# Self attentions of a two-block decoder: split low-precision products against fp32 products with 32 rows a head

## The chip, the cores and the metric

The kernel runs on one core of one Trainium2 chip. The metric is the device time of one launch in microseconds. The engines named below are TensorE (PE, matmuls and transposes; PEld is its weight load), VectorE (DVE), ScalarE (ACT), GpSimd (POOL) and SyncE (SP, which issues most transfers).

## The reference

Two decoder blocks over x of 8 batches x 256 tokens x 256 features, each sublayer followed by a layer norm of the sum with its input: a gated convolution block, a cross attention to 77 context rows, a mixture of experts; then a self attention with rotary positions, a second cross attention, and a last attention with register tokens. The change touches the self attention and the last attention. Both have 16 heads of 16 features.

```python
def _L1_attn_ref(x, w_qkv, w_out, b_out):
    q, k, v = ...                       # (b, 16, 256, 16)
    q, k = _apply_rope(q, cos, sin), _apply_rope(k, cos, sin)
    attn = softmax(einsum('bhsd,bhtd->bhst', q, k) * SCALE)
    return einsum('bhst,bhtd->bhsd', attn, v)... @ w_out + b_out

def _L1_ffn_ref(x, g_info, W_qkv, W_proj, b_proj):
    sim = (qg_n * q_n).sum(-1).mean(-1)           # of the tokens past the first REG = 5
    pos = (sim - sim.min()) / (sim.max() - sim.min()) > 0.9
    def masked_attn(tok_mask):
        l = where(concat([ones(REG), tok_mask]), logits, -inf)
        return einsum('bhqk,bkhd->bqhd', softmax(l), v)
    x_pos, x_neg = masked_attn(pos), masked_attn(~pos)
    reg_out = (x_pos[:, :REG] + x_neg[:, :REG]) * 0.5
    tok_out = where(pos, x_pos[:, REG:], x_neg[:, REG:])
    return concat([reg_out, tok_out]) @ W_proj + b_proj
```

## The kernel before, in words

Even and odd batches are two streams with buffers and four PSUM banks each. `pair(st, i)` is two banks of a stream, `bank(st, i)` one. Every engine's program is written as Python generators, one per stream, and `together` and `beside` (lines 103 to 116) take one piece from each generator in turn. A `yield` or `pause(n)` is the end of a piece, so the places of the yields set the order of each engine's instructions. Engines wait for each other through counted signals with named steps (`sig.up` and `at`). The work goes in stages: x0 (first block up to its cross attention), experts, then `second` for each batch of a stream (`a1`, the self attention; `xattn`; `fq`, which makes queries, keys and values of the last attention and sends them to DRAM), and `fa`, the last attention. Four pairs of batches pass through `second`, then through `fa`.

The self attention `a1` (PE from line 865, ACT 1205, DVE 1596). TensorE turns x, makes queries, keys and values with `mm3` (lines 92 to 95: three products of fp32r high and low parts), VectorE applies the rotation (L1327). `stack` (a ScalarE copy of the high parts, L1006, then VectorE's subtraction for the low parts) lays high and low parts side by side, 48 numbers per head, and one more for minus the row's maximum. TensorE turns two heads at a time (`turn`, transposes at L544), ScalarE copies the result from PSUM. Then `maxima` (L805) multiplies without the maximum, VectorE reduces 128 x 1024 numbers at a time (L1338) and the queries are turned again with the maximum in place. `weigh` takes four groups of two heads for each half of the heads: scores with keys on the partitions (L830), two exponentials of the same scores (L1195 to f16, L1196 to fp32), the low part by subtraction on VectorE (L1327), and 16 small bf16 matmuls with the weights stationary and the values, in three bf16 pieces, moving (L847, L848). VectorE sums the pieces (L1338), inverts and multiplies. `project` turns the result and multiplies with the output weights.

The last attention `fa` (PE 976, ACT 1303, DVE 1748) does the same with two more rows per head for the mask: query and key carry a row of marks each, so that a token sees only its own kind. The five register tokens need both masks. Their second query is made as a block diagonal of 8 columns a head, with maxima (L946), scores (L957, L959), an exponential pair and value products (L971, L972) of their own. `front`, the stacks and turns of the next pair, is interleaved into `weigh` on all three engines.

Lines for prices named later: L606 is an fp32 projection of the context, L662 an fp32 score product of the cross attention in column tiles of 64.

## Time and profile before

| | us |
|---|---|
| median of 3 runs | 2320.46 (2318.49 to 2326.34) |
| the profiled execution | 2325.29, span 2323.5 |
| TensorE matmuls busy | 1759.7 (76%), 12736 records |
| VectorE busy | 1172.5 (50%) |
| ScalarE busy | 918.3 (40%) |
| GpSimd busy | 431.9 (19%) |
| mean granted TensorE clock | 0.792 of full speed |

The profiled execution lies 4.8 us above the median. Its page has a line of 40 slices in which the granted clock is 7 tenths or more in all but one of the first twenty, and 5 to 8 tenths in nineteen of the last twenty (from 1160 us on), which are the rest of the self attention, second cross attention and last attention. A row of the timeline is a run of like instructions: "x16" after a row says that it stands for sixteen, and the bracket names the idle time before it and what ended that. Busy time of TensorE overlaps from one matmul to the next, so spacing of starts is the better measure of its pace.

### The profile page before, as it was taken

How to read it: one execution, taken by the hardware profiler on the slowest of the kernel's cores; microseconds unless marked ns; L12 is line 12 of the kernel's file. 1: busy time of each engine (PE TensorE's matmuls, PEld its weight loads, DVE VectorE, ACT ScalarE, POOL GpSimd, SP SyncE). 2: the span in 40 equal slices, each digit the busy share in tenths (PEclk: the TensorE clock that was granted, in tenths of full speed). 3: DMA queues.
4: the chain of work that ended last, by engine and by line, in shares of the span. 5: the costliest groups of instructions: out<-in, count | busy, mean ns of one | idle time of the engine just before them, and what ended most of it. 6: DMA issues, size and time to landing. Idle time of an engine off the chain costs nothing.

```text
span 2323.5 us, 30395 instructions
## 1 busy us (share of the span) xinstructions
PE 1759.7 (76%) x12736; PEld 1506.3 (65%) x12736; DVE 1172.5 (50%) x2262; ACT 918.3 (40%) x1115; POOL 431.9 (19%) x375
## 2 busy tenths in 40 slices
PE   6685886858799999995686688668767837666666
PEld 6575775656688888884575576557556736555555
DVE  3354443554353333336743754384256436768577
ACT  2443423334322333222641643363236334553735
POOL 1210200102223444432023012302211130000000
PEclk9887888878889999997598676758776866665655
DMA  4000000000300000000000000000000010000000
GB/s 169 1 1 0 1 1 1 1 0 1 163 15 14 28 28 21 8 1 1 1 1 28 1 1 0 28 1 1 28 0 1 1 65 17 28 24 23 1 10 10
DMA packets 8631, 42.14 MB, mean 18 GB/s; under 512 B 1072, under 2 KB 3376, under 8 KB 7472
## 3 DMA queue, kind: packets, MB, share of 16 engines
q1 hardware_dynamic: 8496, 40.21, 4.6%
q8 instruction: 101, 1.65, 0.3%
q14 instruction: 34, 0.28, 0.0%
HBM read 31.82 MB, written 8.39 MB: 17 GB/s over the span
## 4 chain that ended last, share of the span: by engine, by line
PE 56%; DVE 27%; ACT 10%; POOL 3%; issue 3%; DMA 1%; SPq 0%; POOLq 0%; DVEq 0%; ACTq 0%
PE ps L93 12%; PE ps L94 11%; PE ps L95 11%; DVE m L1327 10%; PE ps L544 7%; DVE sm L1338 5%; ACT r L1006 4%; DVE m L1338 4%; PE ps L662 4%; PE ps L606 2%; PE ps L612 2%; DVE m L1335 2%; ACT m L1006 2%; POOL sm L1909 2%; DVE r L1327 1%
## 5 line engine op out<-in xcount | busy, mean ns | idle before, releaser
L544 PE MATMUL ps<-cst,m 128*128 128x128 f32 (+2 forms) x1408 | 249.8, 347 | 150.6 <-POOL m L1823 53.3
L1006 ACT ACTIVATE r<-ps 128x512 fp32r<-128x512 f32 (+2 forms) x232 | 167.2, 748 | 457.4 <-PE ps L544 432.0
L544 PEld LDWEIGHTS ps<-cst,m 128*128 128x128 f32 (+2 forms) x1408 | 215.0, 189 | 191.3 <-POOL m L1823 58.1
L1006 ACT ACTIVATE m<-ps 64x308 f32<-64x308 f32 (+5 forms) x240 | 172.8, 727 | 389.9 <-PE ps L95 227.0
L1327 DVE TENSOR_TENSOR m<-m 128x1024 f16<-128x1024 f32 (+4 forms) x248 | 217.7, 910 | 59.3 <-ACT m L1006 32.7
L1793 POOL TENSOR_SCALAR sm<-sm 128x2 f32<-128x2 f32 x40 | 10.1, 252 | 1163.2 <-DVE sm L1354 1163.2
L1327 DVE TENSOR_TENSOR r<-ps,r 128x512 fp32r<-128x512 f32 x120 | 82.1, 690 | 276.0 <-ACT r L1006 275.8
L1327 DVE TENSOR_TENSOR m<-m,ps 128x1024 f32<-128x1024 f32 (+1 forms) x64 | 71.7, 1120 | 265.7 <-PE ps L95 189.1
L1338 DVE TENSOR_REDUCE sm<-ps 128x68 f32<-128x204 f32 (+2 forms) x208 | 114.9, 555 | 119.6 <-PE ps L646 96.6
L1338 DVE TENSOR_REDUCE m<-ps 128x4 f32<-128x1024 f32 (+1 forms) x144 | 155.0, 1140 | 23.3 <-PE ps L805 20.5
L93 PE MATMUL ps<-r,w0h 128*128 128x256 f32 x448 | 135.1, 302 | 38.7 <-DVE r L1327 38.4
L1858 POOL TENSOR_TENSOR r<-m,r 128x1024 fp32r<-128x1024 f32 x48 | 115.3, 2401 | 263.1 <-ACT r L1006 263.1
L847 PE MATMUL ps<-m 128*128 128x51 bf16 x1024 | 89.0, 205 | 92.2 <-DVE m L1327 89.8
L93 PE MATMUL ps<-xTall,uw 128*128 128x512 f32 x384 | 152.0, 396 | 6.5 <-DVE xres L1327 5.0
L1195 ACT ACTIVATE m<-ps,cst 128x1024 f16<-128x1024 f32 x128 | 152.6, 1193 | 8.5 <-PE ps L830 8.5
L1196 ACT ACTIVATE m<-ps,cst 128x1024 f32<-128x1024 f32 x128 | 153.6, 1200 | 0.0
L94 PE MATMUL ps<-xTall,uw 128*128 128x512 f32 x384 | 151.5, 394 | 0.0
L95 PE MATMUL ps<-xTall,uw 128*128 128x512 f32 x384 | 150.6, 392 | 0.0
L847 PEld LDWEIGHTS ps<-m 128*128 128x128 f16 x1024 | 74.4, 115 | 114.2 <-DVE m L1327 110.5
L93 PE MATMUL ps<-w1h,r 128*128 128x256 f32 (+1 forms) x288 | 103.4, 359 | 50.5 <-DVE r L1327 50.5
L1006 ACT ACTIVATE r<-m 128x1024 fp32r<-128x1024 f32 x64 | 67.8, 1060 | 175.2 <-DVE m L1327 150.5
L94 PE MATMUL ps<-r,w0h 128*128 128x256 f32 x448 | 132.7, 296 | 0.0
(183 smaller groups left out, 4434.4 us busy)
## 6 DMA issues: line engine op xcount, KB each, us to landing
raw<-wu_dram SPq DMA_DIRECT2D x12, 768.0 KB, 4.0
keep_dram<-m SPq DMA_DIRECT2D x8, 768.0 KB, 3.3
m<-keep_dram SPq DMA_DIRECT2D x8, 768.0 KB, 4.3
w1raw<-w_dram SPq DMA_DIRECT2D x1, 3840.0 KB, 14.5
w0raw<-w_dram SPq DMA_DIRECT2D x3, 1024.0 KB, 19.0
w1f<-w1f_dram SPq DMA_DIRECT2D x1, 2048.0 KB, 18.9
out_dram<-xres SPq DMA_DIRECT2D x16, 128.0 KB, 1.8
xres<-x_dram SPq DMA_DIRECT2D x1, 1536.0 KB, 12.9
```

The lines of the kernel that those rows point to most:

```text
L93: pe.matmul(o, l[0], r[0], start=start, stop=False)
L94: pe.matmul(o, l[0], r[1], start=False, stop=False)
L95: return pe.matmul(o, l[1], r[0], start=False, stop=stop)
L544: return pe.transpose(o, i, ident[0:n, 0:n])
L662: m = pe.matmul(bank(st, 2 + g % 2)[r:r + 64, 256 * (hh // 2):256 * (hh // 2) + 256], v.V[:, 64 * h:64 * h + 64], v.PT[g % 2][:, 256 * hh: ...
L847: pe.matmul(ov, hi[:, a, k, js], vv, start=k == 0, stop=False)
L1006: return act.activation(o, i, ACT.Copy)
L1195: act.activation(hv.ph.rearrange("p (a n) -> p a n", a=2), pair(st, i).rearrange("p (a n) -> p a n", a=2), ACT.Exp, scale=scale, bias=lift)
L1196: act.activation(hv.pf, pair(st, i).rearrange("p (a n) -> p a n", a=2), ACT.Exp, scale=scale, bias=lift).then_inc(sig.up(b, f"e{i}{g}"), 1)
L1327: return dve.tensor_tensor(o, a, b_, op)
L1338: return dve.tensor_reduce(o, i, AX.X, op, **kw)
L1858: pool.tensor_tensor(st.r[2][:, 1024:2048], hf, st.r[2][:, 0:1024].bitcast(F32), ALU.subtract).then_inc(st.moe_pool.up(n, k, "lo"), 1)
```

## The change

Both attentions hold queries and keys as plain fp32 in a buffer `QK` with 32 numbers per head: 16 of data, one for minus the maximum (the keys have a one there), two for the mask, zeros. Four heads are turned by one transpose (`turn_heads`), and each head is a tile of 32 rows. `maxima_of` issues eight fp32 matmuls in four row tiles, and VectorE reduces 2048 numbers at once. `attend` takes eight steps of two heads: scores in two row tiles, one exponential to fp32 in one of three buffers `P`; after every second step the values of four heads, stationary, 32 columns wide (16 values, a one for the sum, zeros), in four column tiles with the weights moving. The result has features on the partitions; VectorE copies it (`out_of`), TensorE turns it back (`turn_out`), and `divide` takes one reciprocal and one product. No low parts and no bf16 pieces are left, and no sum over pieces. The first x of both streams is turned before either projection.

The registers' second queries become 8 more columns per head with maxima (L855), scores (L869) and value products (L877) in tiles of 32. In `fa` TensorE and ScalarE no longer interleave the next pair's front; VectorE still does. The generators of `pause(6)` beside the two streams go away on PE and ACT.

```diff
+        def attn_views(v, st, m, r, p, o):
+            v.QK = m[:, 0:2048].rearrange("p (j h n) -> p j h n", j=2, h=32)
+            v.qT, v.kT = (m[:, a:a + 1024].rearrange("p (c n) -> p c n", c=4) for a in (2048, 3072))
+            v.P = [m[:, a:a + 1024] for a in (p, p + 1024, p + 2048)]
...
-                    for a in range(2):
-                        r = 64 * a
-                        for c in range(2):
-                            m = pe.matmul(bank(st, 2 * i + a)[:, c * 256:(c + 1) * 256], qT[r:r + K, 2 * g + c, j * 128:(j + 1) * 128],
-                                          kT[r:r + K, 2 * g + c, :], start=True, stop=True)
...
+            def maxima_of(st, b, v, sig, dve_):
+                for c in range(4):
+                    if c:
+                        pe.wait_ge(*dve_.at(b, f"nm{c - 1}"))
+                    for j in range(2):
+                        for a in range(4):
+                            r = 32 * a
+                            m = pe.matmul(bank(st, a)[:, 256 * j:256 * j + 256], v.qT[r:r + 32, c, 128 * j:128 * j + 128], v.kT[r:r + 32, c, :], start=True, stop=True)
+                    m.then_inc(sig.up(b, f"mx{c}"), 1)
+                    yield
+                pe.wait_ge(*dve_.at(b, "nm3"))
...
-                    for a in range(2):
-                        r = 64 * a
-                        for k in range(2):
-                            m = pe.matmul(pair(st, i)[:, (2 * a + k) * 256:(2 * a + k + 1) * 256], kT[r:r + K, g, k * 128:(k + 1) * 128],
-                                          qT[r:r + K, g, :], start=True, stop=True)
...
-                            for k in range(2):
-                                vv = hv.va[:, k, 2 * g + a, :, :].rearrange("p i n -> p (i n)")
-                                pe.matmul(ov, hi[:, a, k, js], vv, start=k == 0, stop=False)
-                                m = pe.matmul(ov[:, 0:34], lo[:, a, k, js], vv[:, 0:34], start=False, stop=k == 1)
...
+            def attend(st, b, v, sig, act_, dve_, first):
+                def weigh_values(c):
+                    pe.wait_ge(*act_.at(b, f"e{2 * c + 1}"))
+                    if c > 1:
+                        pe.wait_ge(*dve_.at(b, f"ot{c - 2}"))
+                    for k in range(2):
+                        for a in range(4):
+                            w = v.P[(2 * c + a // 2) % 3].rearrange("p (a k n) -> p a k n", a=2, k=2)
+                            m = pe.matmul(bank(st, 2 + c % 2)[32 * a:32 * a + 32, 0:256], v.va[:, k, 4 * c + a, :], w[:, a % 2, k, :], start=k == 0, stop=k == 1)
+                    m.then_inc(sig.up(b, f"o{c}"), 1)
+
+                for u in range(8):
+                    pe.wait_ge(*(act_.at(b, f"e{u - 1}") if u else first))
+                    for k in range(2):
+                        for a in range(2):
+                            r = 64 * (u % 2) + 32 * a
+                            m = pe.matmul(bank(st, a)[:, 256 * k:256 * k + 256], v.kT[r:r + 32, u // 2, 128 * k:128 * k + 128], v.qT[r:r + 32, u // 2, :], start=True, stop=True)
+                    m.then_inc(sig.up(b, f"s{u}"), 1)
+                    if u and u % 2 == 0:
+                        weigh_values(u // 2 - 1)
+                    yield
+                weigh_values(3)
...
+                pe.wait_ge(*act_.at(b, "va"))
+                turn_heads(st, pair(st, 0), v, 16, sig.up(b, "tk"))
+                turn_heads(st, pair(st, 1), v, 0, sig.up(b, "tq"))
+                yield
+                pe.wait_ge(*act_.at(b, "Tq"))
+                yield from maxima_of(st, b, v, sig, dve_)
+                turn_heads(st, pair(st, 1), v, 0, sig.up(b, "t2"))
+                yield
+                yield from attend(st, b, v, sig, act_, dve_, act_.at(b, "T2"))
+                yield
+                pe.wait_ge(*dve_.at(b, "ot3"))
+                turn_out(st, b, v, sig)
+                yield
+                pe.wait_ge(*dve_.at(b, "on"))
+                yield from project_out(st, b, v, pair_of(w1, P1, "wao", 2), sig, dve_)
...
+                pe.wait_ge(*st.f_pool.at("clean"))
+                pe.wait_ge(*dve_.at(b, "f"))
+                turn_heads(st, pair(st, 0), v, 16, sig.up(b, "tk"))
+                turn_heads(st, pair(st, 1), v, 0, sig.up(b, "tq"))
+                yield
+                pe.wait_ge(*act_.at(b, "Tk"))
+                pe.wait_ge(*dve_.at(b, "xq"))
+                for c in range(4):
+                    m = tp(bank(st, 0)[:, 32 * c:32 * c + 8], v.qs[:, 4 * c:4 * c + 4, :].rearrange("p h n -> p (h n)"), 8)
+                m.then_inc(sig.up(b, "xt"), 1)
+                yield
+                pe.wait_ge(*act_.at(b, "xe"))
+                for c in range(4):
+                    for a in range(4):
+                        r = 32 * a
+                        m = pe.matmul(bank(st, a)[32 * c:32 * c + 32, 0:256], v.qx[r:r + 32, c, :], v.kT[r:r + 32, c, :], start=True, stop=True)
+                m.then_inc(sig.up(b, "xm"), 1)
+                yield
+                pe.wait_ge(*dve_.at(b, "nx"))
+                yield from maxima_of(st, b, v, sig, dve_)
+                turn_heads(st, pair(st, 1), v, 0, sig.up(b, "t2"))
+                tp(bank(st, 0)[:, 0:128], v.nx.rearrange("p c n -> p (c n)")).then_inc(sig.up(b, "x2"), 1)
+                yield
+                pe.wait_ge(*act_.at(b, "T2"))
+                pe.wait_ge(*dve_.at(b, "x2"))
+                for k in range(2):
+                    for c in range(4):
+                        for a in range(4):
+                            r = 32 * a
+                            m = pe.matmul(bank(st, a)[:, 32 * k + 8 * c:32 * k + 8 * c + 8], v.kT[r:r + 32, c, 128 * k:128 * k + 128], v.qx2[r:r + 32, c, 0:8], start=True, stop=True)
+                m.then_inc(sig.up(b, "xs"), 1)
+                yield
+                yield from attend(st, b, v, sig, act_, dve_, act_.at(b, "ex"))
+                pe.wait_ge(*act_.at(b, "e7"))
+                for c in range(4):
+                    for k in range(2):
+                        for a in range(4):
+                            m = pe.matmul(bank(st, 0)[32 * a:32 * a + 32, 8 * c:8 * c + 8], v.va[:, k, 4 * c + a, :], v.px[:, a, 32 * k + 8 * c:32 * k + 8 * c + 8], start=k == 0, stop=k == 1)
+                m.then_inc(sig.up(b, "xo"), 1)
+                yield
...
-            def stack(q, qp, kp, sig, b):
-                for j in range(2):
-                    qh = qp[:, j, :, 0:32].rearrange("p h (a n) -> p h a n", a=2).bitcast(F32R)
-                    copy(qh, q[:, j, 0:16, :].unsqueeze(2).to_broadcast([P, 16, 2, 16]))
-                    kh = kp[:, j, :, 0:64].rearrange("p h (a n) -> p h a n", a=2)[:, :, :, 0:16].bitcast(F32R)
-                    copy(kh, q[:, j, 16:32, :].unsqueeze(2).to_broadcast([P, 16, 2, 16])).then_inc(sig.up(b, f"st{j}"), 1)
...
-                    act.activation(hv.ph.rearrange("p (a n) -> p a n", a=2), pair(st, i).rearrange("p (a n) -> p a n", a=2), ACT.Exp, scale=scale, bias=lift)
-                    act.activation(hv.pf, pair(st, i).rearrange("p (a n) -> p a n", a=2), ACT.Exp, scale=scale, bias=lift).then_inc(sig.up(b, f"e{i}{g}"), 1)
...
+            def attend(st, b, v, sig, pe_):
+                for u in range(8):
+                    act.wait_ge(*pe_.at(b, f"s{u}"))
+                    if u > 2:
+                        act.wait_ge(*pe_.at(b, f"o{(u - 3) // 2}"))
+                    act.activation(v.P[u % 3], pair(st, 0), ACT.Exp, scale=0.25).then_inc(sig.up(b, f"e{u}"), 1)
+                    yield
...
+            def maxima_of(st, b, v, sig, pe_):
+                for c in range(4):
+                    dve.wait_ge(*pe_.at(b, f"mx{c}"))
+                    reduce(v.QK[:, :, 4 * c:4 * c + 4, 16].rearrange("p j a -> p a j"), st.ps[:, :].rearrange("p (a j n) -> p a j n", a=4, j=2),
+                           ALU.max, negate=True).then_inc(sig.up(b, f"nm{c}"), 1)
+                    yield
...
+            def out_of(st, b, v, sig, pe_, c):
+                dve.wait_ge(*pe_.at(b, f"o{c}"))
+                dve.tensor_copy(v.OT[:, c, :], bank(st, 2 + c % 2)[:, 0:256]).then_inc(sig.up(b, f"ot{c}"), 1)
...
+            def divide(st, b, v, sig, pe_):
+                dve.wait_ge(*pe_.at(b, "t3"))
+                src = pair(st, 0).rearrange("p (j h n) -> p j h n", j=2, h=16)
+                dve.reciprocal(v.rc, src[:, :, :, 16]).then_inc(sig.up(b, "rc"), 1)
+                dve.wait_ge(*sig.at(b, "rc"))
+                tt(v.o.rearrange("p j (h n) -> p j h n", h=16), src[:, :, :, 0:16], v.rc.unsqueeze(3).to_broadcast([P, 2, 16, 16]), ALU.mult).then_inc(sig.up(b, "on"), 1)
...
+                nxt = front(st, b + 2) if b + 2 < B else iter(())
+                for u in range(8):
+                    if u % 2:
+                        next(nxt, None)
+                    elif u:
+                        out_of(st, b, v, sig, pe_, u // 2 - 1)
+                    yield
```

TensorE at the front and the weighing of a self attention (ps0 and ps1 are the PSUM of the two streams, m30 and m31 their working buffers, r30 and r31 the fp32r ones). Before, at the end of the maxima:

```order
L805 MATMUL ps0<-r30 128x256 x4
L805 MATMUL ps1<-r31 128x256 x4
L544 MATMUL ps0<-cst,m30 128x128 x8
L544 MATMUL ps1<-cst,m31 128x128 x8
L544 MATMUL ps0<-cst,m30 128x128 x8
L544 MATMUL ps1<-cst,m31 128x128 x8
L830 MATMUL ps0<-r30 128x256 x4
L830 MATMUL ps1<-r31 128x256 x4
L830 MATMUL ps0<-r30 128x256 x4
L830 MATMUL ps1<-r31 128x256 x4
L847 MATMUL ps0<-m30 128x51
L848 MATMUL ps0<-m30 128x34
```

The change, from the last maxima on:

```order
L741 MATMUL ps0<-m30 128x256 x8
L741 MATMUL ps1<-m31 128x256 x8
L486 MATMUL ps0<-cst,m30 128x128 x8
L486 MATMUL ps1<-cst,m31 128x128 x8
L762 MATMUL ps0<-m30 128x256 x4
L762 MATMUL ps1<-m31 128x256 x4
L762 MATMUL ps0<-m30 128x256 x4
L762 MATMUL ps1<-m31 128x256 x4
L762 MATMUL ps0<-m30 128x256 x4
L754 MATMUL ps0<-m30 32x256 x8
L762 MATMUL ps1<-m31 128x256 x4
L754 MATMUL ps1<-m31 32x256 x8
```

The 32 transposes between maxima and weighing have become 16, the scores (L830, now L762) keep groups of four, and sixteen matmuls of 51 and 34 columns have become eight of 256 columns for twice as many heads.

ScalarE at the same place, from the copies of the turned x (r30 and r31, 128 x 512) on. Before:

```order
L1006 ACTIVATE r30<-ps0 128x512
L1006 ACTIVATE r31<-ps1 128x512
L1006 ACTIVATE m30<-m30 128x16x32
L1006 ACTIVATE m30<-m30 128x32x16
L1006 ACTIVATE m30<-m30 128x16x32
L1006 ACTIVATE m30<-m30 128x32x16
L1006 ACTIVATE m31<-m31 128x16x32
L1006 ACTIVATE m31<-m31 128x32x16
L1006 ACTIVATE m31<-m31 128x16x32
L1006 ACTIVATE m31<-m31 128x32x16
L1006 ACTIVATE m30<-ps0 128x32x16
L1006 ACTIVATE m30<-m30 128x32x16
```

The change:

```order
L897 ACTIVATE r30<-ps0 128x512
L897 ACTIVATE r31<-ps1 128x512
L897 ACTIVATE m30<-ps0 128x32x16
L897 ACTIVATE m31<-ps1 128x32x16
L897 ACTIVATE m30<-ps0 128x1024 x2
L897 ACTIVATE m31<-ps1 128x1024 x2
L897 ACTIVATE m30<-ps0 128x1024
L897 ACTIVATE m31<-ps1 128x1024
L1066 ACT_TABLE_LOAD
L1066 ACTIVATE m30<-ps0 128x1024
L1066 ACTIVATE m31<-ps1 128x1024
L1066 ACTIVATE m30<-ps0 128x1024
```

The eight stack copies (128x16x32 and 128x32x16) are gone, one value copy a stream is left, and from L1066 on exponentials of the two streams alternate singly.

TensorE ahead of the last attention's maxima and behind them. The change, from the turns of keys and queries on:

```order
L486 MATMUL ps0<-cst,m40 128x128 x16
L486 MATMUL ps1<-cst,m41 128x128 x16
L486 MATMUL ps0<-cst,m40 128x8 x4
L486 MATMUL ps1<-cst,m41 128x8 x4
L855 MATMUL ps0<-m40 32x256 x16
L855 MATMUL ps1<-m41 32x256 x16
L741 MATMUL ps0<-m40 128x256 x8
```

...and behind the maxima:

```order
L741 MATMUL ps0<-m40 128x256 x8
L741 MATMUL ps1<-m41 128x256 x8
L486 MATMUL ps0<-cst,m40 128x128 x9
L486 MATMUL ps1<-cst,m41 128x128 x9
L869 MATMUL ps0<-m40 128x8 x32
L869 MATMUL ps1<-m41 128x8 x32
L762 MATMUL ps0<-m40 128x256 x4
L762 MATMUL ps1<-m41 128x256 x4
```

Before, the registers' transposes and maxima (L946) stood between maxima of the tokens; now L855 precedes the maxima and 64 matmuls of 8 columns (L869) stand between the second turns and the first scores.

## Rows read from the trace of the kernel before

**Rows 1.** The page: span, and the chain that ended last by engine.
```profile
span 2323.5 us, 30395 instructions
...
PE 56%; DVE 27%; ACT 10%; POOL 3%; issue 3%; DMA 1%; SPq 0%; POOLq 0%; DVEq 0%; ACTq 0%
```

**Rows 2.** Windows: us, busy PE, PEld, DVE, ACT, POOL (instructions), granted clock, DMA share, GB/s.
```profile
1255.00:1296.00 41.00, 21.15 (x120) 18.39 (x120) 18.21 (x37) 13.95 (x21) 12.82 (x16) 0.75 0.05 20
1296.00:1315.00 19.00, 14.00 (x79) 10.06 (x80) 18.00 (x16) 2.26 (x3) 0.00 (x0) 0.57 0.00 1
1315.00:1353.00 38.00, 23.56 (x340) 19.56 (x339) 30.01 (x63) 35.09 (x35) 0.00 (x0) 0.59 0.00 1
2020.00:2048.00 28.00, 18.93 (x126) 16.17 (x123) 26.00 (x31) 3.20 (x7) 1.76 (x3) 0.63 0.00 0
2048.00:2115.00 67.00, 42.51 (x552) 36.74 (x550) 41.51 (x98) 49.88 (x58) 0.00 (x0) 0.66 0.11 33
```

**Rows 3.** Chain of waits, self attention of the second pair: start us, us, what.
```profile
1299.28 12.54 DVE m L1338 x11
...
1311.86 3.69 PE ps L544 x16
...
1318.49 1.00 ACT m L1195
...
1319.50 1.01 ACT m L1196
...
1352.82 1.10 PE ps L544 x4
```

**Rows 4.** Groups by line and shape: count, busy us, mean ns, idle before.
```profile
L1338 DVE TENSOR_REDUCE m<-ps 128x4 f32<-128x1024 f32 x128 | 146.6, 1212 | 20.6 <-PE ps L805 20.5
...
L662 PE MATMUL ps<-m 77*64 77x256 f32 x512 | 86.4, 481 | 0.0
```

**Rows 5.** Timeline ahead of a self attention: start us, us, what [idle <-releaser].
```profile
1266.31 0.79 PE L93 MATMUL ps<-w1h,r 128*128 128x512 f32 x1 [8.62 <-DVE r L1327]
...
1274.89 1.88 DVE L1327 TENSOR_TENSOR m<-ps,cst 128x1024 f32<-128x1024 f32 x3
...
1276.80 0.69 DVE L1327 TENSOR_TENSOR m<-m 128x512 f32<-128x512 f32 x1
...
1279.05 2.19 ACT L1006 ACTIVATE m<-m 128x512 fp32r<-128x512 f32 x4 [4.86 <-DVE m L1327]
...
1297.00 3.49 DVE L1338 TENSOR_REDUCE m<-ps 128x4 f32<-128x1024 f32 x3 [5.42 <-PE ps L805]
```

**Rows 6.** Timeline of TensorE, end of the maxima of another pair.
```profile
1109.96 0.80 PE L805 MATMUL ps<-r 49*128 49x256 f32 x4 [0.33 <-DVE m L1338]
...
1111.10 5.23 PE L544 MATMUL ps<-cst,m 128*128 128x128 f32 x32 [0.34 <-DVE m L1338]
```

**Rows 7.** Timeline of TensorE, cross attention, first pair.
```profile
1210.16 1.10 PE L544 MATMUL ps<-cst,m 128*77 128x128 f32 x8
1211.18 1.08 PE L662 MATMUL ps<-m 77*64 77x256 f32 x8
```

**Rows 8.** The same instructions of the second pair.
```profile
1410.81 1.99 PE L544 MATMUL ps<-cst,m 128*77 128x128 f32 x8
1412.73 1.98 PE L662 MATMUL ps<-m 77*64 77x256 f32 x8
```

**Rows 9.** Timeline, fp32 projection of the context.
```profile
1159.96 3.59 PE L606 MATMUL ps<-w1f,ctxT 128*77 128x512 f32 x8
```

**Rows 10.** Timelines, last attention: a first reduction, two first maxima, 16-column matmuls.
```profile
1916.58 1.22 DVE L1338 TENSOR_REDUCE m<-ps 128x4 f32<-128x1024 f32 x1
...
2019.69 0.51 PE L805 MATMUL ps<-r 51*128 51x256 f32 x4
...
2124.39 0.60 PE L805 MATMUL ps<-r 51*128 51x256 f32 x4
...
2053.47 1.88 PE L959 MATMUL ps<-r 128*128 128x16 f32 x8
```

599 lines of the change are left out of this document (156 added, 443 removed).

## The prediction

> **What bounds the kernel now.** I read the page first, then the stages that the change touches in a table of windows, then the chain of waits, then single rows for prices. The page's chain is 56% TensorE and 27% VectorE over 2323.5 us [rows 1]: no engine is the bound everywhere, so each edit has to be priced in its own stage. The program runs two streams (even and odd batches), and four pairs of batches pass through the self attention one after the other, later through the last attention. The stages of the second pair's self attention [rows 2] are: before the maxima (1255 to 1296, ending with dependent copies of ScalarE and VectorE), the maxima (1296 to 1315, VectorE busy for 18.00 of 19.00: it is the bound), and the weighing (1315 to 1353, ScalarE 30.01 and VectorE 35.09 of 38.00, TensorE waiting). The chain agrees: eleven reductions follow each other at 12.54 / 11 = 1.14 us, then 16 transposes, then exponentials of 1.0 us each in couples [rows 3]. The weighing runs from 1317.3 (1311.86 + 3.69 of transposes and a copy) to 1352.82 [rows 3]: 35.5 us for a pair. The last attention takes 104.7 us from pair to pair (2019.69 to 2124.39 [rows 10]); the three steps from the first maxima at 1914.0 to the last at 2229.9 average 105.3.
>
> The third thing to see is TensorE's clock: 0.75, 0.57 and 0.59 granted in these three stages, 0.63 and 0.66 in the last attention [rows 2]. Matmul durations show its two levels (2.4 and 1.2 GHz): the same 8 transposes and 8 fp32 matmuls take 1.10 and 1.08 us in the first pair [rows 7], 1.99 and 1.98 in the second [rows 8]. After the change TensorE has more to do in the weighing than any other engine, so this level decides how much is gained.
>
> **Price of an fp32 matmul.** L662 is written 256 times and has 512 records [rows 4]: an fp32 matmul is two passes. Eight records of 512 columns took 3.59 us [rows 9], 0.449 each; by start spacing 0.43 for 512 columns, so 0.216 for 256 columns at the fast level, and 0.43 at the slow one. L662 puts two column tiles side by side: 8 records of 256 columns in 1.08 us [rows 7] are four slots of 0.27 with the last one's tail, 1.98 when slow [rows 8]. I price the new matmuls as if four tiles of 32 rows (or of 32 columns) also ran together; no row of before shows four, so that is a rival below.
>
> **Self attention, per pair.**
> (a) Ahead of the maxima. The hi/lo stacks go: four ScalarE copies of 2.19 us a stream [rows 5] and four subtractions behind them, the value splits, 32 of the 64 transposes ahead of the maxima and four of their eight copies. In the row of now, the rotation's products of stream 0 start at 1274.89 and the first reduction at 1297.00 [rows 5]. New: projection of stream 0 from 1266.31 [rows 5] to 1272.4 (it begins at the slow level, 0.43 between starts of 512 columns, and ends at the fast), that of stream 1 directly behind instead of after its own x, to 1276.6, two rotations of 1.88 + 0.69 + 1.47 + gaps = 4.3 one after the other to 1281, 16 transposes (2.2 with some at the slow level), copy, first maxima: 1285.0. **-12.0.** The new copies on ScalarE (values and turned heads, 1.0 to 1.1 each) lie beside TensorE's transposes.
> (b) Maxima. 8 reductions of 2048 elements instead of 16 of 1024 at 1.14. I take 2.2 (between 2.14 and 2.28, the fixed part is small): 17.6 for 18.1. **-0.5.** TensorE needs 4 slots of 0.43 = 1.7 when slow, less than 2.2: hidden behind VectorE.
> (c) Second turn: 16 transposes for 32. **-0.6.**
> (d) Weighing. Now TensorE, in a fixed order of eight steps a stream. One step's scores are 4 matmuls, 8 passes, two at a time: 0.865 fast, 1.71 slow. The values of two steps are 8 matmuls, 16 passes, four at a time: 0.865 or 1.71. Fast: a step without values is limited by its own loop, scores 0.865, exponential 1.0 and handovers, two streams: 2.35; a step with values is TensorE's, 4 x 0.865 = 3.46; with 0.6 for the changes of tile shape 6.4 for two steps, four times 25.7. Slow: 3.42 + 6.84 + 0.6 = 10.9, four times **43.4**. Against 35.5: **-9.8 fast, +7.9 slow.** One exponential for two (8 x 2 x 1.0 fewer per pair), the f16 subtractions (1.2 each) and the 512 small matmuls are gone, but only down to TensorE's own time.
> (e) Tail: eight transposes a stream, reciprocal and one product before the projection: **+2.5.**
> Sum: -20.4 fast, -2.7 slow. Four pairs: -82 or -11.
>
> The changes of tile shape in (d) have this row: 8 transposes from 1210.16 at 0.107 would end at 1211.02 and L662 begins at 1211.18 [rows 7]: 0.16 for a change. The Trainium skill says the same in kind ("TensorEngine Tiling (Array Packing)"): a change of the tiling mode drains TensorE; the 0.16 is this trace's price. It is a rule against this change, which alternates shapes 12 to 16 times a pair: 2.4 us, counted above.
>
> **Last attention, per pair.** Before prefetches the next pair's front under the weighing on every engine; after does it on VectorE alone, so TensorE and ScalarE run the whole cycle in a row. Slow level: 32 transposes (6.8), copy, register transposes and register maxima until VectorE can reduce 10.4; maxima 17.6; second turn (18 a stream for 16), the 64 score matmuls of 8 columns, one small exponential 8.8; weighing 43.4; 64 value matmuls of the registers 5.7; 18 transposes 4.0; divisions and register rows 4.3, gap 0.8; transposes, projection 5.1. For the tiny matmuls the nearest row is a full-size tile's: 16 columns took 1.88 / 8 = 0.235 each [rows 10]. In four tiles the 64 (128 passes) would be 3.8 by the instruction and 7.5 by the pass; I take the first, since their weights are a quarter of that tile's, and keep the second, twice 3.7 a pair, 30 in all, for the range. Sum 100.1 against 105.3: -5.2, three times. The first one begins 2.1 earlier (first reduction at 1916.58 [rows 10], stack gone), the last has nothing prefetched to save it: 95.5 for 93.0, +2.5. All slow: **-15**; each fast weighing -17.7 more, all fast: **-86**.
>
> **Which level.** The granted clock rises and falls with how closely matmuls follow each other, and in the new order TensorE has few gaps in the weighing if it is at the slow level (10.3 of 10.9) and more if it is fast (5.2 of 6.4). Before, where the waits are longer (23.56 of 38.00 busy), the clock was 0.59 [rows 2]. What decides is the level at entry. Behind the maxima stand 32 transposes in a row: the same sort of transposes start at slow spacing and finish at fast in [rows 6] (32 in 5.23, mean 0.163, between 0.107 and 0.213), though four-matmul bursts with gaps of 0.33 in 1.13 came before. In the new order 16 follow maxima of which TensorE is busy 1.7 of 2.2, so I expect three of four self attentions fast. In the last attention 64 tiny matmuls stand between them and the weighing; I expect one of four fast. So 3 x -17.7 - 11 = -64 and -17.7 - 15 = -33: **-97 against the profiled 2325.3, 2228.** The profiled execution is 4.8 over the median of 2320.46, so **2223.**
>
> The Trainium skill ("TensorE: Matmul & The Clock Gate", Part 4) says that transposes do not bring the fast clock. The trace disagrees [rows 6]: nothing but transposes ran there while their spacing fell. By the page the first rival below holds. The same page (Part 3) gives 3.07 instead of 4 for four row tiles of 32: about an estimated 2 us a pair more, none of it in the sum.
>
> **Rivals.**
> 1. All weighings slow: 2325.3 - 11 - 15 = 2299, median 2294. For it: 0.57 to 0.66 in all these stages now [rows 2]. Against: [rows 6].
> 2. All fast: 2325.3 - 82 - 86 = 2157, median 2152. For it: the new stages are busier than before's; against: the 0.63 and 0.66, and the tiny matmuls.
> 3. **Slower:** tiles of 32 run only two at a time, at the slow level. Then maxima need 3.4 a step instead of VectorE's 2.2, +9.8 a pair, and the values 3.4 instead of 1.7, 4 x 2 x 1.71 = +13.7; in the last attention the registers' three groups +12 more. 8 x 23.5 + 4 x 12 = 236 on 2299: 2535, median 2530. It decides only together with the slow level: at the fast one the maxima still hide behind VectorE and the values cost 8 x 6.9 + 24 = 79, giving 2236. For it: no row shows four tiles. Against: [rows 7, 8] show that two share a slot exactly.
> 4. The fixed order of the two streams misfits (a stream waits behind the other's wait for an exponential, VectorE's front of the next pair delays the copies of the outputs): 5 to 10 us a pair, which takes most of the gain, 2300 to 2350.
>
> **How the numbers follow.** Forecast 0.55, rival 1 0.17, rival 2 0.13, rival 3 0.08, rival 4 0.07. Predicted 2223; the forecast's own spread is 17.7 per weighing that changes level, so 2170 to 2260 with the tiny matmuls' upper bound. The range 2150 to 2300 takes in rivals 1 and 2 and leaves out rival 3, part of 4, 0.13 in all. About 0.3%, 7 us, is what a measurement can tell from no change. Faster: the first three and a little of rival 4, 0.87; same 0.03; slower, rival 3 and the upper part of 4, 0.10.
>
> **What would show it.** The first reduction of the second pair 12 to 13 us after the rotation's first product instead of 22; reductions of 2048 elements at 2.2 with little idle time; eight single exponentials a stream; the weighing 26 or 43 long, nothing in between, by the spacing of its matmuls; last cycles of 100 or 82. It is wrong if the eight maxima matmuls of a step take 3.4 when slow, if VectorE or ScalarE waits on the other stream inside a weighing, or if the level changes inside one.

## The result, and the profile after

| | before | after |
|---|---|---|
| median of four runs, us | 2323.4 (2318.49 to 2329.06) | 2193.85 (2177.62 to 2194.68) |
| ratio after / before | | 0.9425, 95% interval 0.9375 to 0.9475 |
| profiled execution, us | 2325.29 | 2193.69 |
| mean granted TensorE clock | 0.792 | 0.839 |

The change makes the kernel 5.75% faster (interval 5.25 to 6.25%). Profiled execution against profiled execution it is -131.6 us; the prediction had -97, and a median of 2223 where 2193.85 was measured. Page of the changed kernel, the rows that answer to [rows 1]:

```profile
span 2191.7 us, 29840 instructions
...
PE 67%; DVE 22%; ACT 5%; issue 3%; POOL 2%; DMA 1%; SPq 0%; POOLq 0%; DVEq 0%; ACTq 0%
```

TensorE holds 67% of the chain instead of 56, ScalarE 5% instead of 10. The new groups by line and shape (count, busy us, mean ns, idle before), which answer to [rows 4]:

```profile
L762 PE MATMUL ps<-m 32*128 32x256 f32 x1024 | 194.8, 552 | 3.1 <-ACT m L1066 2.8
L1169 DVE TENSOR_REDUCE m<-ps 128x8 f32<-128x2048 f32 x64 | 142.7, 2286 | 13.6 <-PE ps L741 13.0
L1066 ACT ACTIVATE m<-ps 128x1024 f32<-128x1024 f32 x128 | 130.0, 1023 | 139.1 <-PE ps L762 138.6
...
L754 PE MATMUL ps<-m 128*32 128x256 f32 x1024 | 98.9, 525 | 0.8 <-ACT m L1066 0.8
```

The rows of before that they are to be compared with:

```profile
L1195 ACT ACTIVATE m<-ps,cst 128x1024 f16<-128x1024 f32 x128 | 152.6, 1193 | 8.5 <-PE ps L830 8.5
...
L847 PE MATMUL ps<-m 128*128 128x51 bf16 x1024 | 89.0, 205 | 92.2 <-DVE m L1327 89.8 <-ACT r L1006 2.4
```

ScalarE spends 130 us on exponentials where it spent 306 (152.6 here and 153.6 on their fp32 twins), and is idle ahead of them for 139 instead of 8.5, released by TensorE's scores. TensorE was idle for 92.2 us ahead of the value products, nearly all of it until VectorE's subtractions were done; now it waits for exponentials 3.6 us in the whole kernel. The order of wait has turned round.

Now the stages, as in [rows 2] (us, busy PE, PEld, DVE, ACT, POOL with instructions, granted clock, DMA share, GB/s): the maxima and the weighing of the second self attention, the cross attention behind it; then, of the first pair of the last attention, what lies ahead of the weighing and the weighing itself.

```profile
1297.00:1318.00 21.00, 14.47 (x147) 9.74 (x145) 17.77 (x8) 2.05 (x2) 0.00 (x0) 0.83 0.00 1
1318.00:1344.00 26.00, 25.12 (x261) 14.85 (x260) 3.18 (x8) 17.07 (x17) 0.00 (x0) 1.00 0.01 2
1396.00:1413.00 17.00, 16.89 (x122) 11.88 (x123) 8.27 (x16) 13.09 (x17) 4.79 (x5) 0.89 0.00 1
1835.00:1863.00 28.00, 22.01 (x276) 16.81 (x274) 20.30 (x13) 2.43 (x3) 0.00 (x0) 0.71 0.01 1
1863.00:1906.00 43.00, 43.00 (x340) 25.23 (x344) 5.58 (x24) 16.77 (x17) 0.00 (x0) 0.51 0.10 37
```

The same instructions take 25.6 us at a granted clock of 1.00 (2.4 GHz) and 43.3 at 0.51 (nearly all at 1.2 GHz), TensorE busy almost from end to end. "Fast" and "slow" are used below for these two levels. The eight weighings, first score to last value product: **42.6, 25.6, 25.6, 25.6** in the self attentions, **43.3, 43.3, 43.4, 43.5** in the last attention. Two pieces of the chain of waits (start us, us, what), first in the second self attention, then in the last attention, show where each goes:

```profile
1321.52 2.21 PE ps L762 x16
1323.73 1.00 PE ps L754 x16
1324.73 1.06 PE ps L762 x8
```

```profile
1884.04 2.01 PE ps L762 x8
1886.05 1.87 PE ps L754 x16
1887.92 5.21 PE ps L762 x24
```

A stream's scores of a step (8 records) take 1.06 or 2.01, its value products (16 records, four column tiles) 1.00 or 1.87. Four tiles of 32 do run side by side: one after the other, 16 records at the prediction's 0.216 would take 3.5 at the fast level.

Cut at the same instructions, the second pair compares like this. All marks are starts of TensorE instructions: first maxima, first score, the transposes that end the weighing, the ones at the head of the cross attention's weighing, its last ones, the x of the next self attention, the next maxima.

| stage, us | before | after | |
|---|---|---|---|
| maxima and second turn | 20.9 | 20.7 | -0.2 |
| weighing | 35.5 | 25.6 | -9.9 |
| to the cross attention | 47.4 | 47.6 | +0.1 |
| cross attention | 49.4 | 35.7 | **-13.7** |
| last projection | 20.0 | 20.6 | +0.6 |
| front of the next self attention | 38.8 | 26.1 | -12.7 |
| pair | 212.1 | 176.3 | -35.8 |

The largest term is in the cross attention, whose code the change doesn't touch. Its window of before, below, holds one TensorE instruction more than that of after (the third window above) and differs in the clock, 0.50 against 0.89:

```profile
1405.00:1434.00 29.00, 28.88 (x123) 18.47 (x124) 8.61 (x16) 13.47 (x17) 4.81 (x5) 0.50 0.00 1
```

It doesn't take over the level of the weighing. Between weighing and cross attention the clock is 1.00 in either case: behind the slow weighing of the first pair, behind the fast one of the second, and in the kernel before.

```profile
1158.00:1205.00 47.00, 41.24 (x295) 35.41 (x292) 21.63 (x39) 15.71 (x25) 9.37 (x12) 1.00 0.01 1
1344.00:1392.80 48.80, 42.44 (x303) 36.38 (x301) 23.38 (x42) 16.43 (x26) 9.85 (x13) 1.00 0.00 1
```

```profile
1360.10:1400.90 40.80, 35.98 (x258) 30.86 (x257) 17.32 (x28) 15.01 (x24) 9.43 (x12) 1.00 0.00 1
```

It falls to 0.50 at the head of every cross attention, where TensorE has two waits of 3.4 to 3.8 us, and what differs is how long it stays there: 6.8 us in the second pair of after, 37.5 in that of before.

The whole last attention takes 357.0 us from its first maxima to the end (2191.7 - 1834.7), 409.5 before.

### The profile page after: what moved, and what is told of

Same layout as the page of the kernel before. It is cut to its first block, busy times and chain, and to the rows that moved or that the text cites. A ratio compares the mean times of both kernels' runs of the same rounds, so it can differ in the third digit from the quotient of the medians.

```text
span 2191.7 us, 29840 instructions
## 1 busy us (share of the span) xinstructions
PE 1787.6 (82%) x13024; PEld 1439.5 (66%) x13024; DVE 918.1 (42%) x1710; ACT 690.1 (31%) x830; POOL 432.8 (20%) x371
## 4 chain that ended last, share of the span: by engine, by line
PE 67%; DVE 22%; ACT 5%; issue 3%; POOL 2%; DMA 1%; SPq 0%; POOLq 0%; DVEq 0%; ACTq 0%
PE ps L93 13%; PE ps L94 12%; PE ps L95 12%; PE ps L762 8%; DVE m L1169 7%; PE ps L486 7%; PE ps L754 4%; DVE m L1158 4%; PE ps L604 4%; DVE sm L1169 3%; PE ps L548 3%; PE ps L554 3%; DVE m L1166 3%; ACT m L897 2%; DVE r L1158 1%
## 5 line engine op out<-in xcount | busy, mean ns | idle before, releaser
L897 ACT ACTIVATE m<-ps 128x1024 f32<-128x1024 f32 (+6 forms) x296 | 220.7, 761 | 637.7 <-PE ps L95 264.1
L486 PE MATMUL ps<-cst,m 128*128 128x128 f32 (+2 forms) x1136 | 187.3, 323 | 121.7 <-POOL m L1621 52.7
L486 PEld LDWEIGHTS ps<-cst,m 128*128 128x128 f32 (+2 forms) x1136 | 155.2, 174 | 163.5 <-POOL m L1621 57.4
L762 PE MATMUL ps<-m 32*128 32x256 f32 x1024 | 194.8, 552 | 3.1 <-ACT m L1066 2.8
L762 PEld LDWEIGHTS ps<-m 32*128 32x128 f32 x1024 | 129.9, 267 | 67.1 <-issue 32.4
L1066 ACT ACTIVATE m<-ps 128x1024 f32<-128x1024 f32 x128 | 130.0, 1023 | 139.1 <-PE ps L762 138.6
L1169 DVE TENSOR_REDUCE m<-ps 128x8 f32<-128x2048 f32 (+1 forms) x72 | 152.1, 2167 | 25.4 <-PE ps L741 13.0
L93 PE MATMUL ps<-xTall,uw 128*128 128x512 f32 x384 | 153.6, 400 | 10.2 <-DVE xres L1158 8.7
L897 ACT ACTIVATE r<-ps 128x512 fp32r<-128x512 f32 x120 | 70.7, 597 | 235.8 <-PE ps L486 215.1
L95 PE MATMUL ps<-r,w0l 128*128 128x256 f32 x448 | 132.1, 295 | 0.0
L741 PE MATMUL ps<-m 32*128 32x256 f32 x1024 | 96.5, 504 | 40.3 <-DVE m L1169 38.9
L93 PEld LDWEIGHTS ps<-r,w0h 128*128 128x128 f32 x448 | 91.9, 205 | 42.1 <-DVE r L1158 40.7
## 6 DMA issues: line engine op xcount, KB each, us to landing
xres<-x_dram SPq DMA_DIRECT2D x1, 1536.0 KB, 12.7
```

The lines of the kernel that those rows point to most:

```text
L93: pe.matmul(o, l[0], r[0], start=start, stop=False)
L95: return pe.matmul(o, l[1], r[0], start=False, stop=stop)
L486: return pe.transpose(o, i, ident[0:n, 0:n])
L741: m = pe.matmul(bank(st, a)[:, 256 * j:256 * j + 256], v.qT[r:r + 32, c, 128 * j:128 * j + 128], v.kT[r:r + 32, c, :], start=True, stop=True)
L762: m = pe.matmul(bank(st, a)[:, 256 * k:256 * k + 256], v.kT[r:r + 32, u // 2, 128 * k:128 * k + 128], v.qT[r:r + 32, u // 2, :], start=Tru ...
L897: return act.activation(o, i, ACT.Copy)
```

## The experiments

Twelve runs were made in three groups, each group on one chip and beside the kernel before; the ratios are to that. "Weighings" are the eight times as above, four of the self attention | four of the last attention.

**1. Transposes ahead of the last attention's weighing.**

```diff
                 m.then_inc(sig.up(b, "xs"), 1)
                 yield
+                pe.wait_ge(*act_.at(b, "ex"))
+                for _ in range(16):
+                    tp(bank(st, 3)[:, 0:128], ident)
                 yield from attend(st, b, v, sig, act_, dve_, act_.at(b, "ex"))
```

> The changed kernel, and in the last attention, between the registers' small exponential and the first scores, 16 more transposes of the identity per stream on TensorE, whose result nobody reads. Theory A: the weighing of the last attention is slow (43.4 us against 25.6 in three of the self attentions) because the 64 matmuls of 8 columns ahead of it let the clock fall, and a weighing keeps the level it starts with. Then the transposes cost 4 to 5 us a pair, the weighing falls to 25.6, and the time goes from 2194 to about 2142 (4 times -13). Rival B: the last attention's weighing is slow for a reason of its own (the masks' front on VectorE, what runs in it). Then the time rises by 4 x 5 to about 2213 and the weighings stay at 43.

Measured: 2172.85, ratio 0.9325 (0.9257 to 0.9394). Weighings 42.6, 25.6, 25.6, 25.6 | 27.9, 30.4, 42.8, 30.4; the profiled execution took 2155. Three of four changed level through work that nobody reads (their 27.9 and 30.4 include the second stream's transposes). The third did not: the clock rose 1.1 us into it and was back at half from 7.9 us on. A rules over B, but not every time.

**2. The small matmuls ahead of the self attention's weighing.**

```diff
+                pe.wait_ge(*act_.at(b, "T2"))
+                for k in range(2):
+                    for c in range(4):
+                        for a in range(4):
+                            r = 32 * a
+                            pe.matmul(bank(st, a)[:, 32 * k + 8 * c:32 * k + 8 * c + 8], v.kT[r:r + 32, c, 128 * k:128 * k + 128], v.qT[r:r + 32, c, 0:8], start=True, stop=True)
+                yield
                 yield from attend(st, b, v, sig, act_, dve_, act_.at(b, "T2"))
```

> The changed kernel, and in the self attention, between the second turn of the queries and the first scores, the same 32 matmuls of 8 columns per stream that the last attention has there, with the result unread. Theory A: the three fast weighings become slow, +17.7 each, the cross attentions behind them partly too (+7 each), and the small matmuls cost 3 to 5 us a pair: 2194 + 53 + 20 + 16 = 2283. Rival B: only their own cost, 2194 + 16 = 2210, weighings stay at 25.6.

Measured: 2270.46, ratio 0.9753 (0.9703 to 0.9803). Weighings 42.3, 43.4, 42.2, 43.4 | 44.2, 43.9, 43.9, 43.9. Windows of the second weighing and of the cross attention behind it:

```profile
1318.00:1362.00 44.00, 44.00 (x284) 25.28 (x281) 2.97 (x7) 16.38 (x16) 0.00 (x0) 0.50 0.00 1
1418.00:1443.00 25.00, 25.00 (x108) 14.85 (x107) 5.32 (x9) 10.29 (x13) 2.65 (x3) 0.50 0.00 1
```

None of the four weighings takes 25.6 any more. The two experiments together show it from both sides: the same weighing takes either time, by what TensorE did just ahead of it.

**3. The registers' scores moved ahead of the maxima.** No work is added; the order of TensorE, ScalarE and VectorE changes. Below is TensorE's part, and ScalarE's and VectorE's follow it.

```diff
-        FPE = ["tk", "tq", "xt", "xm", *MX, "t2", "x2", "xs", *SPE, "xo", "t3", "oT", "y"]
+        FPE = ["tk", "tq", "xt", "xm", "x2", "xs", *MX, "t2", *SPE, "xo", "t3", "oT", "y"]
...
                 pe.wait_ge(*dve_.at(b, "nx"))
-                yield from maxima_of(st, b, v, sig, dve_)
-                turn_heads(st, pair(st, 1), v, 0, sig.up(b, "t2"))
                 tp(bank(st, 0)[:, 0:128], v.nx.rearrange("p c n -> p (c n)")).then_inc(sig.up(b, "x2"), 1)
                 yield
-                pe.wait_ge(*act_.at(b, "T2"))
                 pe.wait_ge(*dve_.at(b, "x2"))
...
-                yield from attend(st, b, v, sig, act_, dve_, act_.at(b, "ex"))
+                pe.wait_ge(*act_.at(b, "ex"))
+                yield from maxima_of(st, b, v, sig, dve_)
+                turn_heads(st, pair(st, 1), v, 0, sig.up(b, "t2"))
+                yield
+                yield from attend(st, b, v, sig, act_, dve_, act_.at(b, "T2"))
```

> The changed kernel with the registers' score matmuls (8 columns) and their exponential moved ahead of the maxima of the last attention, so that only transposes stand between maxima and weighing, as in the self attention. No work is added. Theory A: all four weighings of the last attention at 25.6 instead of 43.4, with 2 us a pair lost on VectorE's two waits before the maxima: 2194 - 4 x 15.8 = 2131. Rival B: 2194 + 8 = 2202.

Measured: 2145.2, ratio 0.9227 (0.9176 to 0.9279), and again on another chip:

> The same program as xs_early, as the base of the next two on this chip: 2135 to 2156. Under both theories the first weighing of each attention may come out slow (42 to 44) or fast (26), 17 us apart.

2149.84, ratio 0.9202 (0.9156 to 0.9247). Weighings 43.7, 25.6, 25.6, 25.6 | 42.1, 26.4, 26.2, 26.2 (in the second run of it within 0.1 the same). Two windows of the last attention, its first and its second weighing:

```profile
1845.00:1887.00 42.00, 41.90 (x320) 23.46 (x322) 6.27 (x25) 17.41 (x17) 0.00 (x0) 0.55 0.10 39
1936.00:1963.00 27.00, 26.12 (x382) 16.21 (x383) 6.54 (x26) 17.08 (x17) 0.00 (x0) 1.00 0.25 80
```

**This version beats both kernels**, the changed one by about 2% (ratio 0.9227 and 0.9202 against 0.9425, each to the kernel before on its own chip; the two were not run side by side). Three of the last attention's four weighings became fast; a fast cycle of the last attention is 75.2 us from maxima to maxima, against 88.7 of the changed kernel and 105.3 before.

**4. A second exponential in each step of the self attention.**

```diff
-            def attend(st, b, v, sig, pe_):
+            def attend(st, b, v, sig, pe_, again=None):
                 for u in range(8):
                     act.wait_ge(*pe_.at(b, f"s{u}"))
                     if u > 2:
                         act.wait_ge(*pe_.at(b, f"o{(u - 3) // 2}"))
+                    if again is not None:
+                        act.activation(again, pair(st, 0), ACT.Exp, scale=0.25)
                     act.activation(v.P[u % 3], pair(st, 0), ACT.Exp, scale=0.25).then_inc(sig.up(b, f"e{u}"), 1)
...
-                yield from attend(st, b, v, sig, pe_)
+                yield from attend(st, b, v, sig, pe_, st.r[3][:, 1024:2048])
```

> The changed kernel with a second exponential of the same scores in every step of the self attention, into an unused buffer. If TensorE bounds the weighing with little to spare, as the sum has it (6.4 us for two steps when fast), four exponentials of 1.02 us a step of both streams make ScalarE the bound at 8.2: 25.6 becomes 33 in the three fast pairs, the slow one stays near 43: +22, 2216; more if the longer waits let the clock fall (each such pair +10 and its cross attention +7). Rival: the exponentials were never in the way and it costs nothing, 2194.

Measured: 2272.34, ratio 0.9754 (0.9701 to 0.9807). Weighings 47.7, 45.9, 46.6, 45.9: not the 33 of a ScalarE bound. The timeline of TensorE in the second weighing (start us, us, what, idle before and its releaser):

```profile
1313.37 2.31 PE L762 MATMUL ps<-m 32*128 32x256 f32 x16
...
1316.54 1.13 PE L762 MATMUL ps<-m 32*128 32x256 f32 x8 [0.85 <-ACT m L1068]
...
1318.37 3.91 PE L762 MATMUL ps<-m 32*128 32x256 f32 x16 [0.70 <-ACT m L1068]
...
1322.21 1.94 PE L754 MATMUL ps<-m 128*32 128x256 f32 x16
```

It begins at the fast spacing, waits 0.85 and 0.70 us for the doubled exponentials, and is at the slow one 5 us in, where it stays to the end. So the level at entry is not the whole rule. The other three begin at 1.00 as well and fall 3.1 to 4.7 us in.

**5. The same with 16 transposes a stream ahead of it** (`tp(bank(st, 0)[:, 0:128], ident)` behind the second turn).

> two_exp with 16 transposes of the identity per stream right behind the second turn of the queries in the self attention. Theory A (a weighing keeps the level it starts with): all four weighings of the self attention at the fast level, where ScalarE bounds them at 33 us instead of 46: 2272 + 16 for the transposes - 52 - 15 in the cross attentions = 2221. Theory C (the level follows the waits inside the weighing; two_exp's weighings began at the fast spacing of 108 ns and fell after 5 us, while TensorE waited for the doubled exponentials): they fall again, 46 us each, and the transposes cost 3 to 4 us a pair: 2286.

Measured: 2262.57, ratio 0.9692 (0.9661 to 0.9723). Weighings 46.2, 46.2, 46.2, 46.2, with cross attentions behind them of 15.6 each. The windows of the transposes, the first steps and the rest, in the second pair:

```profile
1311.00:1318.00 7.00, 6.76 (x60) 6.47 (x62) 2.38 (x2) 2.24 (x3) 0.00 (x0) 1.00 0.00 0
1318.00:1324.00 6.00, 3.60 (x24) 2.07 (x24) 0.00 (x0) 6.00 (x7) 0.00 (x0) 0.87 0.00 0
1324.00:1362.00 38.00, 37.00 (x220) 18.95 (x220) 2.97 (x7) 24.19 (x26) 0.00 (x0) 0.50 0.00 1
```

Theory A falls and C's forecast holds: the clock is 1.00 at entry, TensorE is busy 3.60 of the next 6.00 us, and from there on the clock is 0.50 although TensorE is then busy for 37 of 38. Its being busy does not bring the level back here.

**6. 8 transposes a stream behind the second turn in the first pair of each attention** of the version of experiment 3.

```diff
                 turn_heads(st, pair(st, 1), v, 0, sig.up(b, "t2"))
+                if b < 2:
+                    for _ in range(8):
+                        tp(bank(st, 0)[:, 0:128], ident)
```

> xs_early, and in the first pair of each attention 8 transposes of the identity per stream, result unread, right behind the second turn of the queries, where TensorE otherwise waits for ScalarE's copy. Theory A: the two weighings that were slow in xs_early (43.7 and 42.1 us, the first of each attention) start at the fast level and hold it: 2 x -17 + 2 x 1.5 for the transposes: about 2145 - 31 = 2114. Rival: these first weighings are slow for what came long before (their maxima at the slow level) and 16 transposes are too little: 2148.

Measured: 2142.39, ratio 0.9207 (0.9131 to 0.9284), the same as without. Weighings 41.6, 25.6, 25.6, 25.6 | 26.2, 43.4, 26.2, 26.2. The last attention's first one became fast, its second slow.

**7. The same in all pairs.**

> xs_early with the 8 transposes per stream behind the second turn in all pairs of both attentions, not the first ones alone. Theory A: all eight weighings fast, 8 x 1 for the transposes, two weighings (17 each) gained over xs_early: 2145 + 8 - 30 = 2123. Theory C: the first weighings stay a matter of chance, since TensorE's waits in the first two steps are what they were: 2150.

Measured: 2189.32 over four runs that lie between 2145.29 and 2219.56, too far apart for a verdict. The profiled one (2145.29) has 41.6, 41.0, 25.6, 25.6 | 26.2, 26.2, 26.2, 26.2.

**8. 32 transposes a stream in the first pairs.**

> xs_early with 32 transposes per stream (64 in a row, 7 us fast, 13 slow at the most) ahead of the first weighing of each attention. Theory A: the first weighings are fast in every run: -34, and the transposes cost 10 to 14: 2145 - 22 = 2123. Theory C: they begin fast and fall in some runs all the same: 2145 to 2160.

Measured: 2156.77, ratio 0.9252 (0.9208 to 0.9295). Weighings 25.6, 25.6, 25.6, 25.6 | 42.2, 43.4, 26.2, 26.2. The first self attention, 41.6 to 43.9 in every other profile with single exponentials, came down to 25.6; the last attention's first two are slow. Experiments 6 to 8 give nothing over experiment 3: what the transposes win in one weighing is lost by their own time or by another weighing that falls.

**9. The kernel before, with 8 transposes a stream and half ahead of its weighings.**

```diff
                 hi, lo = (w.rearrange("p (a k n) -> p a k n", a=2, k=2) for w in (hv.ph, hv.pl))
+                for _ in range(8):
+                    tp(pair(st, i)[:, 0:128], ident)
                 yield from pause(i)
```

> The kernel before, with 8 transposes of the identity per stream and half of the heads ahead of the scores of both attentions (32 a pair), result unread. Theory A: there the weighing waits for ScalarE and VectorE, so the fast level does not hold and would bring little: weighings stay at 35 to 36 us, and the transposes cost 3 to 7 us a pair: 2323 + 40 = 2363. Rival: the gain of the change is the clock that before could have had as well: the weighing and the cross attention behind it speed up and pay for the transposes, 2323 or less.

Measured over ten runs: 2313.04, ratio 0.9941 (0.99 to 0.9983): faster than before by 0.6% (0.2 to 1.0), a small gain, but with 256 useless transposes in it. The weighing stays near 35 (36.0, 34.9, 34.9, 34.9, as theory A had it), but the cross attentions behind it take 13.6, 15.6, 15.6, 13.9 where they took 13.6, 24.5, 21.9, 15.7. The second one:

```profile
1421.00:1438.00 17.00, 17.00 (x113) 10.86 (x113) 5.57 (x9) 10.90 (x15) 2.88 (x3) 0.82 0.00 1
```

The rival is right for the part of the gain that lies in the cross attention: before could have had it. How the transposes do it isn't shown: as before, the clock is at 1.00 for 41 us between weighing and cross attention and falls at its head, but in the second pair it stays down for 13.7 us instead of 37.5.

**10. Value products tile by tile.**

```diff
-                    for k in range(2):
-                        for a in range(4):
+                    for a in range(4):
+                        for k in range(2):
                             w = v.P[(2 * c + a // 2) % 3].rearrange("p (a k n) -> p a k n", a=2, k=2)
```

> The changed kernel, the eight value matmuls of a group issued column tile by column tile (both key halves of one tile next to each other) instead of round the four tiles. If tiles run side by side only when neighbours in the queue are of different tiles, a group takes 5 matmul times instead of 2: +1.3 us fast, +2.6 slow, 8 groups a pair: +10 in the three fast weighings, +21 in the five slow ones: 2194 + 30 + 105 = 2329, all of the change's gain. Rival: TensorE overlaps them however they are ordered: 2194.

Measured: 2185.11, ratio 0.9374 (0.9306 to 0.9441), not to be told from the changed kernel. Weighings 43.9, 25.8, 25.8, 25.8 | 43.4, 43.5, 43.5, 43.6. The rival holds: the order of the tiles in the queue is worth 0.2 us.

**11. Each stream's projection directly behind its own x**, as in before.

```diff
                 turn_x(st, b, sig)
-                yield
                 qkv(st, b, wao, sig, dve_)
+                yield
                 yield
                 yield
```

> The changed kernel with the order of before at the head of the self attention: each stream's projection directly behind its own turned x, so that the second stream's x is turned after the first one's projection. The second projection then waits for its x to be split (0.6 + 0.6 + 0.7 us) as it did before: +2 us a pair, 2194 + 8 = 2202, if the second projection is on the path. Rival: the rotations on VectorE (4.3 us each, one after the other) hide it: 2194.

Measured: 2195.77, ratio 0.9408 (0.9325 to 0.9491), which alone says nothing. In the trace the second and third pair take 181.1 and 180.9 us from maxima to maxima, in the changed kernel 176.3 and 178.7: 2 to 5 us a pair for this part of the front, in the direction of the sum.

## Why the prediction was right, and where it wasn't

The measured time lies in the range, and the mechanism is the forecast's. The number owes something to luck: the gain is 131.6 us where 97 were forecast, and this holds a miss of 17.7 in one direction and two of 38.8 and 13.2 in the other, which partly cancel. The steps in turn:

- **The weighing.** 25.7 fast and 43.4 slow were predicted, 25.6 and 43.3 to 43.5 measured. Prices from the cross attention's fp32 matmuls and the assumption of four tiles at once were right, and rival 3 (two at a time) is out. (L662, called a score product ahead, is the cross attention's value product with the values stationary; its price stands.) The number of slow weighings was guessed right for the self attentions, three of four fast, and wrong for the last attention: none of four instead of one, +17.7.
- **The front.** -12.0 predicted, -12.7 measured: from the first product of the projection to the turns of the keys 7.9 less, from there to the maxima 5.0 less. The first reduction of the second pair comes 13.3 us after the rotation's first product, where 12 to 13 were forecast.
- **Maxima.** A reduction of 2048 elements starts every 2.2 us, as assumed, but the stage saves 0.2, not 1.1: the second stream's turn still waits for the last reduction.
- **Tail.** +2.5 predicted, +0.1 measured up to the cross attention. The transposes and the division are there: from the end of the weighing to the output projection it is 4.3 us for 2.5, +1.8. But the 24 products of that projection then took 3.0 instead of 5.0, because before's clock stayed at half until 1360 us, 7 us behind its weighing:

```profile
1353.00:1360.00 7.00, 6.54 (x30) 5.90 (x30) 3.60 (x10) 1.19 (x2) 0.00 (x0) 0.50 0.01 2
```

- **What was priced at nothing: the cross attention.** Its weighing took 13.6, 24.5, 21.9, 15.7 before and 20.1, 13.0, 13.7, 13.1 after: -16 together, and nothing of that was in the sum. Over the twelve profiles of the changed kernel and its variants, all 27 cross attentions behind a weighing of 25.6 to 25.8 us took 13.0 to 13.8; the 21 behind one of over 40 us took anything from 13.0 to 24.5. This is not a level handed on: ahead of all 48 the clock was at 1.00 for 47 us or more, and fell within 1.6 us of the head. Why a fast weighing is always followed by a short fall isn't shown.
- **The last attention outside the weighing.** The sum had 56.7 us for it, all at the slow level; 45.3 were measured (88.7 - 43.4). In the second cycle the registers' value products, 5.7 in the sum by no row, leave TensorE 0.7 us behind the weighing (-5.0); the 32 transposes of the next pair's front run at the fast spacing (3.7 for 6.8) and so do the 18 behind the weighing (2.2 for 4.0). The registers' scores are not among the savings: 64 matmuls, 128 records, take 4.6, where the sum took 3.8 and kept 7.5 for the range. (Its "18 a stream" for the second turn is 18 a pair, nine a stream, as its 8.8 needs.) Rows of the timeline: these scores for both streams, the values of one stream, the 18 transposes.

```profile
1946.72 4.82 PE L869 MATMUL ps<-m 32*128 32x8 f32 x128
...
1992.80 0.98 PE L877 MATMUL ps<-m 128*32 128x8 f32 x64
...
1995.17 2.19 PE L486 MATMUL ps<-cst,m 128*128 128x128 f32 x18
```

  Over four pairs this is 395.8 predicted (3 x 100.1 + 95.5) against 357.0. (The cycles of 100 or 82 that the prediction names came out at 88.7, and at 75.2 in experiment 3.)

The three misses add up: -97 + 17.7 (level) - 38.8 (last attention) - 13.2 (to its first maxima, where the cross attentions are) = -131.3, measured -131.6.

**The step that failed in its reasoning** is "what decides is the level at entry". Experiments 1 and 2 fit it, 4 and 5 break it: there all eight weighings with doubled exponentials enter at 1.00 and fall 3.1 to 5.9 us in, while TensorE waits for ScalarE. The prediction named a level that changes inside a weighing as a sign that it is wrong, and this happened in the changed kernel itself, in the first pair:

```profile
1115.10:1119.70 4.60, 3.35 (x27) 2.21 (x28) 0.00 (x0) 4.24 (x4) 0.00 (x0) 1.00 0.02 4
1119.80:1157.20 37.40, 37.40 (x229) 20.37 (x230) 2.97 (x7) 14.32 (x14) 0.00 (x0) 0.50 0.00 0
```

The trace of before showed it too. Its weighings also begin at 1.00 and fall after some 5 us; the second one:

```profile
1317.30:1322.40 5.10, 2.09 (x33) 1.57 (x32) 1.22 (x1) 5.10 (x7) 0.00 (x0) 1.00 0.00 0
1322.50:1352.80 30.30, 18.99 (x288) 15.64 (x289) 28.39 (x61) 28.16 (x29) 0.00 (x0) 0.50 0.00 1
```

Over the twelve profiles, 88 weighings have single exponentials. Of the 56 at 1.00 as they begin, 43 stay fast and 13 fall 1.0 to 5.2 us in; of the 32 at half, 30 come out slow, and two of experiment 1 come back 5 us in, with the second stream's transposes behind their first scores. So both the level at entry and the first steps count.

This changes what the single exponential is worth. The expectation of experiment 4 had 33 us for a fast weighing with two, an estimated 7 more; measured were 45.9, 20 more, since none stayed fast. The step between the levels alone, as single exponentials show it, is 17.7 (25.6 to 43.3).

The rule of the Trainium skill that was weighed ("TensorE: Matmul & The Clock Gate", Part 4, transposes don't bring the fast clock) is not borne out. In experiment 8 TensorE ran nothing but transposes from 1111.3 to 1122.3, and the clock rose among them, at 1115.65; the weighing behind them is the first one of a self attention that came out fast:

```profile
1108.00:1115.60 7.60, 7.28 (x48) 5.68 (x41) 5.45 (x3) 1.02 (x1) 0.00 (x0) 0.50 0.00 0
1115.70:1122.00 6.30, 6.30 (x60) 6.30 (x59) 0.00 (x0) 2.31 (x2) 0.00 (x0) 1.00 0.01 3
```

By that rule of the Trainium skill the median would have been 2294; it was 2194.

**Left open:** why the first weighing of each attention comes out slow in experiment 3 and its second run alike (in all four the clock is at 1.00 in its first microseconds and falls 3.3 to 4.3 in), and which of the waits in the first two steps decides. The 2177.62 among the changed kernel's runs lies 16 us below the other three, about what one weighing's change of level is worth; that execution wasn't profiled. What the rest of the front's -12.7 owes to the stacks and what to fewer transposes wasn't tried apart.

## What to carry to other kernels

Where TensorE becomes the bound, its time has two prices here, a factor of 1.7 apart, and what stands ahead of the stage and a few waits of under a microsecond in its first steps decide which. Keep tiny matmuls away from the head of a long TensorE stage, keep its first steps free of waits, and look at the granted clock of each window rather than at busy time. Count also the stages behind the edited one: their code is the same, but their clock can move, as that of the cross attentions did here. When a stage can settle at either level, test it with dummy transposes first, then get the same effect by reordering real work: here that was worth about a third of the change itself.

## What was not expected of the hardware

- The clock does not come back while TensorE is kept busy by these 32-row and 32-column matmuls: 0.50 over 38 us with TensorE busy for 37 (experiment 5), and 0.51 over 43 of 43 in the changed kernel, while the same matmuls hold 1.00 over the 26 us of a fast weighing. In the slow ones it rises within 2 us of the weighing's end.
- Neighbours in the queue need not be of different tiles: value products ordered tile by tile took the same time (25.8 against 25.6).
- Tiny fp32 matmuls in tiles of 32, two records each: with 8 columns in four row tiles 128 records took 4.82 us, 38 ns each on average; in four column tiles 64 took 0.98, 15 ns each.
- 256 transposes whose result nobody reads made the kernel before 0.6% faster (0.2 to 1.0).
